# A vision block in one launch: where the position rows and vectors are turned, and in which order the first patch products run

## The reference

```python
patches = patchify(x, 16)                                  # (32, 36, 768) from (32, 3, 96, 96)
h = concat([cls, einsum('bnd,ed->bne', patches, W) + b], 1) + pos    # (32, 37, 256)
paths = sigmoid(h @ Wp + bp)                               # 8 heads, depth 5
agree = pq * pk + (1 - pq) * (1 - pk)
sim = cumprod(agree, -1).sum(-1) / 5                       # causal mask, softmax over keys
h = layernorm(h + (softmax(sim) @ (h @ Wv)) @ Wo)
y = silu((norm(h) * gamma + beta) @ dequant(fc1) + fc1_bias)
h = layernorm(h + (h + 0.5 * (y @ dequant(fc2) + fc2_bias)))
```

## Time and profile before

| | us |
|---|---|
| median of 3 runs | 157.21 |
| lowest and highest | 156.9 to 157.31 |
| the profiled execution | 156.75 |
| its span, first to last instruction | 155.0 |
| TensorE matmul busy in the span | 147.8 (95%) |
| VectorE, ScalarE, GpSimd busy | 82.5, 61.8, 48.7 |

### The profile page before, as it was taken

One profiled execution on the slowest core, in us unless ns is written; L12 is line 12 of the kernel. 1 busy time (PEld: TensorE's weight loads), 2 busy tenths in 40 slices (PEclk: granted clock), 3 DMA queues, 4 the chain that ended last, 5 costly groups with the idle time before them and its releaser, 6 DMA issues.

```text
span 155.0 us, 2930 instructions
## 1 busy us (share of the span) xinstructions
PE 147.8 (95%) x1122; PEld 117.5 (76%) x1122; DVE 82.5 (53%) x160; ACT 61.8 (40%) x133; POOL 48.7 (31%) x125
## 2 busy tenths in 40 slices
PE   6899999999999999999999999999999999999970
PEld 5678777767577796778878777887888888878860
DVE  2424186548878853779227597704779125630041
ACT  0531305523243754837468326548316432034200
POOL 5050001303072802646108316403652105630011
PEclk9999999999999999999999999999999999999999
DMA  4999999900000000000100010010010100100001
GB/s 147 285 267 272 254 340 396 400 38 0 0 0 6 4 0 4 0 7 5 34 0 0 4 34 0 0 38 0 0 34 4 34 0 2 34 6 34 0 34 34
DMA packets 5615, 10.67 MB, mean 69 GB/s; under 512 B 748, under 2 KB 4417, under 8 KB 5345
## 3 DMA queue, kind: packets, MB, share of 16 engines
q1 hardware_dynamic: 5146, 10.07, 21.0%
q10 hardware_dynamic: 454, 0.40, 1.0%
HBM read 9.26 MB, written 1.21 MB: 68 GB/s over the span
## 4 chain that ended last, share of the span: by engine, by line
PE 91%; DMA 3%; DVE 2%; issue 1%; SPq 0%; ACT 0%; POOLq 0%; POOL 0%
PE bank_s L566 21%; PE bank_z L598 18%; PE bank_z L460 8%; PE bank_p L475 4%; PE bank_s L503 4%; PE bank_w L518 4%; PE bank_s L434 3%; PE bank_p L476 3%; DMA x_rows<-in_x 3%; PE bank_o L537 3%; PE bank_o L538 3%; PE bank_w L522 3%; PE bank_p L449 2%; PE bank_w L598 2%; PE bank_z L449 2%; PE bank_w L449 2%
## 5 line engine op out<-in xcount | busy, mean ns | idle before, releaser
L566 PE MATMUL bank_s<-hnT,w 128*128 128x256 f32 (+1 forms) x160 | 32.9, 364 | 0.0
L566 PEld LDWEIGHTS bank_s<-hnT,w 128*128 128x128 f32 x160 | 28.8, 190 | 3.7 <-ACT hnT L751 0.4
L598 PE MATMUL bank_z<-w,act 128*128 128x256 f32 x128 | 30.0, 381 | 0.0
L598 PEld LDWEIGHTS bank_z<-w,act 128*128 128x128 f32 x128 | 23.6, 191 | 3.0
L741 ACT ACTIVATE act<-bank_s,vec_cols 128x256 f32<-128x256 f32 (+1 forms) x40 | 16.1, 454 | 18.5 <-PE bank_s L566 18.5
L348 POOL TENSOR_TENSOR rstd<-var,exponents 128x3 f32<-128x3 f32 (+1 forms) x10 | 8.7, 871 | 36.3 <-DVE var L869 36.2
L856 DVE RECIPROCAL recip<-bank_w 128x222 f32<-128x222 f32 (+1 forms) x11 | 16.4, 1494 | 1.0 <-PE bank_w L522 1.0
L863 DVE BATCH_NORM_STATS2 stats<-bank_o 128x6 f32<-128x256 f32 (+1 forms) x10 | 4.3, 430 | 18.4 <-PE bank_o L538 18.2
L723 ACT ACTIVATE phi_q<-bank_p 128x222 f32<-128x222 f32 (+1 forms) x11 | 3.9, 351 | 24.8 <-PE bank_p L485 24.8
L460 PE MATMUL bank_z<-xT,wT 128*128 128x288 f32 x48 | 13.1, 417 | 0.0
L733 ACT ACTIVATE probs<-bank_s 111x888 f32<-111x888 f32 (+1 forms) x11 | 9.8, 888 | 6.6 <-PE bank_s L503 6.6
(11 more groups left out here) (114 smaller groups left out, 230.7 us busy)
## 6 DMA issues: line engine op xcount, KB each, us to landing
x_rows<-in_x SPq DMA_DIRECT2D x5, 576.0 KB, 10.3
q<-in_L_ffn_fc_q SPq DMA_DIRECT2D x2, 1024.0 KB, 17.8
s<-in_L_ffn_fc_scales SPq DMA_DIRECT2D x2, 1024.0 KB, 20.2
out<-fin SPq DMA_DIRECT2D x9, 128.0 KB, 1.7
x_rows<-in_x SPq DMA_DIRECT2D x2, 288.0 KB, 4.4
w_rows<-in_L_tok_W SPq DMA_DIRECT2D x2, 256.0 KB, 6.2
w_rows<-in_L_tok_W ACTq DMA_DIRECT2D x1, 256.0 KB, 2.9
wvp<-in_L_attn_Wv SPq DMA_DIRECT2D x1, 256.0 KB, 7.8
```

Of the source, the lines that this page charges most:

```text
L566: last = mm(block[:, i], w1[:, e, f * 128:(f + 1) * 128], hnT[p % 2][:, e, 0:n], start=(e == 0), stop=(e == E2 - 1))
L598: last = mm(z_bank(b)[0:w, 0:D], act2[:, f, in_pair(b)], w2[:, f, :], start=(f == 0), stop=(f == FB - 1))
```

## The change

It does six things.

- `turn_vectors` moves from behind the second channel's products into block 0: after the fillers "before the second half" and before the wait for that half's rows. Those fillers go from 5 to 2.
- The four small transposes write bank_w (`vec_bank`) and no longer a part of bank_s. The first product into bank_w now waits until VectorE has read them (`posb_step`); the wait for that in block 3 goes.
- On VectorE `position_columns` and `class_tokens` move from behind block 2's copy to behind block 0's copy, before block 1 is regrouped.
- The two position loads move from SyncE's queue to ScalarE's, between the first weights and the vector loads. The three bias loads and the fc2 bias load go behind ScalarE's copy of block 0 (`later_loads`).
- `first_products` replaces `project_channel(0, 0)`: K chunk 0 for both output halves, then K chunk 1 for both.
- The third weight turn stands between the two output halves of channel 1's first chunk, no longer behind both.

TensorE around block 0, before. L398 are fillers, L406 turns weights, L434 turns patches, L449 multiplies.

The diff, cut to its core:

```diff
-    KEEP_BUSY = {"before the weights": 10, "before the first half": 4, "before the second half": 5}
+    KEEP_BUSY = {"before the weights": 10, "before the first half": 4, "before the second half": 2}
-        vec_bank = bank_s[:, 1, 3 * HR:512]
+        vec_bank = bank_w
...
-            sp.dma_start(pos_rows[0:32], pos_flat[0:32]).then_inc(pos_in, 16)
-            sp.dma_start(pos_rows[32:T], pos_flat[32:T]).then_inc(pos_in, 16)
...
                 pe.wait_ge(weight_set, 5)
-                pe.wait_ge(xT_dve, C)
...
                         keep_busy("before the second half" if ih else "before the first half")
+                        if ih == 1:
+                            turn_vectors()
                     pe.wait_ge(x_pat_ready, n + 2 if n > 0 else ih + 1)
-                    if n == C and ih == 0:
-                        pe.wait_ge(posb_step, 1 + E2)
...
+                        if n == 0 and c == 1 and e == 1 and k == 0:
+                            pe.wait_ge(posb_step, 1 + E2)
...
+            def first_products():
+                pe.wait_ge(wT_ready, 1)
+                for k in range(2):
+                    pe.wait_ge(xT_act if k else xT_dve, 1)
+                    for e in range(E2):
+                        mm(first_half_bank(0, e)[:, 0:CP], wT[:, k, e * 128:(e + 1) * 128], patches(k, 0),
+                           start=(k == 0), stop=False)
...
-            project_channel(0, 0)
+            first_products()
             turn_weight(1)
             project_channel(0, 1, outputs=(0,))
             turn_block(1)
             project_channel(0, 1, outputs=(1,))
-            project_channel(1, 0)
+            project_channel(1, 0, outputs=(0,))
             turn_weight(2)
+            project_channel(1, 0, outputs=(1,))
             turn_block(2)
             project_channel(1, 1)
-            turn_vectors()
             project_channel(2, 0)
...
             act.dma_start(w_rows[:, :, 0:256], w_by_channel[0]).then_inc(w_in[0], 16)
+            act.dma_start(pos_rows[0:32], pos_flat[0:32]).then_inc(pos_in, 16)
+            act.dma_start(pos_rows[32:T], pos_flat[32:T]).then_inc(pos_in, 16)
...
             x_columns(n)
+                if n == 0:
+                    later_loads()
...
             x_columns(0)
+            position_columns()
+            class_tokens()
             by_patch(1)
             x_columns(1)
             by_patch(2)
             x_columns(2)
-            position_columns()
-            class_tokens()
```

More of the change, by code:

```diff
@@ L257, in _ @@
             x_block(2)
-            pos_flat = pos.rearrange("o t d -> (o t) d")
-            sp.dma_start(pos_rows[0:32], pos_flat[0:32]).then_inc(pos_in, 16)
-            sp.dma_start(pos_rows[32:T], pos_flat[32:T]).then_inc(pos_in, 16)
             sp.dma_start(wvp[:, :, 0:D], Wv.rearrange("(e p) n -> p e n", p=128)).then_inc(wvp_in, 16)
@@ L678, in _ @@
             act.dma_start(w_rows[:, :, 0:256], w_by_channel[0]).then_inc(w_in[0], 16)
+            pos_flat = pos.rearrange("o t d -> (o t) d")
+            act.dma_start(pos_rows[0:32], pos_flat[0:32]).then_inc(pos_in, 16)
+            act.dma_start(pos_rows[32:T], pos_flat[32:T]).then_inc(pos_in, 16)
             for i, vec in enumerate((tok_b.rearrange("(e p) -> e p", p=128),
@@ L684, in _, with later_loads @@
             act.dma_start(vec_rows[4 * E2:N_VEC], fc1_bias.rearrange("(f p) -> f p", p=128)).then_inc(vec_in, 16)
-            act.wait_ge(bias_step, 1)
-            for part in range(PARTS):
-                act.dma_start(bias_f[32 * part:32 * part + 1], bp.rearrange("(o n) -> o n", o=1)).then_inc(bias_in, 16)
             act.preload_act_table(ACT.Exp)
-            act.dma_start(b2[:], fc2_bias.rearrange("(o n) -> o n", o=1).broadcast_to([128, D])).then_inc(b2_in, 16)
+            def later_loads():
+                act.wait_ge(bias_step, 1)
+                for part in range(PARTS):
+                    act.dma_start(bias_f[32 * part:32 * part + 1], bp.rearrange("(o n) -> o n", o=1)).then_inc(bias_in, 16)
+                act.dma_start(b2[:], fc2_bias.rearrange("(o n) -> o n", o=1).broadcast_to([128, D])).then_inc(b2_in, 16)
             def weight_columns(c):
```

## The result

| | before | changed |
|---|---|---|
| median | 157.26 us (4 runs, 156.9 to 157.5) | 161.66 us (4 runs, 160.45 to 162.22) |
| ratio | 1 | 1.0271, interval 1.024 to 1.0302 |
| span of the profiled execution | 155.0 us | 159.8 us |
| mean granted TensorE clock | 0.999 | 0.978 |

The forecast was 157.3, within 156.0 to 158.5. The time lies outside: 3.2 us above the upper end. The medians differ by 4.40 us, the two profiled executions (156.75 and 161.52) by 4.77; what follows is read from those two.

The account below looks back on a forecast made before the run. TensorE was taken as the bound almost everywhere (91% of the chain). Savings of -1.59 us and +1.71 us for the vectors' new place summed to +0.1 us on the median 157.21: 157.3 us, wide range 156.0 to 158.5.

Parts of the forecast that it names:

- First products by K chunk: First products on TensorE: chunk 0 to both banks first covers ScalarE's copy; 1.94 us instead of 2.42, -0.48.
- Third weight turn: Before block 2's second half: a product between turn and block covers ScalarE's 0.60 us weight copy, -0.46.
- Vectors out of the old place: TensorE before block 3: 0.45 us of transposes and 0.20 us on the product behind them go, -0.65.
- Vectors in the new place: Inside block 0: TensorE waits for loads usable at 8.1, so the second half starts at 8.65, not 6.94: +1.71.
- bound by the issue: Landing of the last vector load: issue at 3.98 plus 3.1 plus 0.55 makes it usable at 7.65.
- bound by the place on the queue: Last vector load, now eighth on ScalarE's queue: packets end about 7.95, usable at 8.5.
- The clock: Block 0: TensorE's idle hole lowers its clock, 2 to 3 us of work slow; +1.3, 158.6; chance 0.09.
- rival 2: Block 0: loads come late, usable at 9.24, second half starts at 9.8; net +1.3, 158.5; chance 0.17.
- Rival 1: Block 0: loads come early, usable at 7.3 or sooner; gain 0.7 to 1.6, about 156.2; chance 0.26.
- Rival 4: First products or third weights: holes stay unfilled, up to 0.9 us remain, 158.1; chance 0.04.
- VectorE, bias loads, rigid shift: VectorE's position work before block 1 and later bias loads are hidden, no cost; everything behind block 3 shifts rigidly.

Follow-up runs that it names:

- e3: Kernel before with both reorderings (first products by K chunk, third weight turn moved), vectors and loads where they were: 156.56 us, ratio 0.9948.
- e1: Kernel before with only the first products run K chunk by K chunk: 156.89 us, ratio 0.9973.
- e4: Changed kernel with 33 fillers instead of 2 ahead of the turned vectors: 159.3 us, ratio 1.0118.
- e2: Kernel before with only the third weight turn moved between the two output halves: 156.61 us, ratio 0.9952.
- e6: Changed kernel, but SyncE waits for the vector loads before issuing the second image block and everything behind it: 157.71 us, ratio 1.0037.
- e8: Changed kernel with vectors turned ahead of block 1, VectorE regrouping block 1 first, five fillers back: 156.22 us, ratio 0.9930.
- e9: Changed kernel, but the two position loads are issued by SyncE right behind block 0's halves: 156.07 us, ratio 0.9942.
- e7: Changed kernel with the five vector loads ahead of the two position loads on ScalarE's queue: 163.1 us, one execution only.

## Why the prediction was wrong, step by step

- **First products by K chunk, -0.48.** The wait between the chunks went, as said. Alone the step is worth 0.26 (e3) to 0.39 us (e1), since the first product takes longer than 0.485 where it starts behind a break; in e4 it comes right behind other work, takes 0.52, and the term nearly holds (2.42 - 1.98 = 0.44).
- **Third weight turn, -0.46.** Right to the hundredth (e2).
- **Vectors out of the old place, -0.65.** Right with the others: the three terms were to give 1.59 and gave 1.67 (e4).
- **Vectors in the new place, +1.71: the step that failed.** Its working said usable at 8.1 between 7.65 and 8.5; it was 10.13, although the load was issued 0.43 us sooner than counted. Two terms of it were mis-sized. The last packet ran at about 8.7, not at 7.1 to 7.95: the bound by the issue used a load that was through before the 6 KB rows came, and e6 shows that these decide. The bound by the place on the queue came nearer, but was still 0.75 us short of the last packet, and I took the middle towards the other one. And the 0.55 us from last packet to use, read from one load, was 1.4 here. The load made 3.24 + 0.52 = 3.76 us where 1.71 stood.
- **The clock, a rival with 9 in 100 at +1.3.** It was the right mechanism at too low a chance and half its size: 2.81 us, where the sum had nothing. I took 2 to 3 us of work to run slow; the trace shows 6.0 us of it, from 10.18 to 16.2. The argument against it, that the smaller hole of before did nothing, said nothing on a longer one. That the first ten fillers ran at the lower level I read from their speed alone, since the profile's clock reads 1.00 there; the slow stretch fits the reading, with 1.15 us for six patch transposes against 0.65 in e4. And its chance hung on the size of the hole: had I taken the hole of rival 2, usable at 9.24 or later, the two would not have been separate cases. Both came, and the sum of both lay outside a range made from either alone.
- **Rival 1** (usable at 7.3 or sooner): the load took 6.6 us in the changed kernel, and 3.6 us with the bulk rows held back. (The 2.0 us of fixed cost that the Trainium skill's page "DMA: Bandwidth & Descriptors" gives in its section "Anatomy of one DMA — SWDGE (gpsimd) path" did not carry over to this queue, with bulk transfers beside it or without; the page gives them for loads issued by GpSimd, and no run here has one.)
- **Rival 2** (usable at 9.24, net +1.3): right in kind. The load came later still, at 10.13, and this rival had no clock in it.
- **Rival 4** did not happen: neither saving was lost, though the first came out smaller alone (above).
- **VectorE, bias loads, rigid shift:** right. The hidden steps stayed hidden, and block 3 to the end took 133 us in both.

The miss is so large because two errors have one origin: the hole was longer than counted, and in the longer hole the clock fell.

## What to carry to other kernels

A wait moved forward in the line of the engine that bounds the kernel costs what the slowest of its loads costs at the new time, and the price of a load of 4 KB was not its bytes but what shared the DMA engines with it (6.58 or 3.59 us): place tiny loads so that they are through before bulk rows start, or put their first use behind work that covers the landing. A long stand of TensorE was paid twice here, in waiting and in clock, so treat "late" and "slow clock" as one case, not as two rivals. Enough fillers hold the clock but not the time (e4, 159.3 us); useful products ahead of the wait hold both (e8, 156.22 us). And read the spread and the clock of all executions, not only at the one profiled: e9's profile shows nothing of its three long ones.

## What the runs showed of the hardware that I had not expected

- A 4 KB load issued at 3.55 us took 6.58 us to be usable while 6 KB rows were moving, and 3.59 us without them (e6). From last packet to use it took 0.55 us in one case and 1.4 in another; why is open.
- The granted clock fell in a hole of 3.44 us in the changed kernel and after less than 2 us of standing in e7, and came back in the changed kernel only after about 6 us of unbroken work. A hole of 0.70 us left it at 1.00 in the profiled execution of e9, and so did 33 identity transposes in a row (e4).
